# Preparation of a test-time-training layer: both channel swaps by on-chip transfers, the sine table in PSUM, key stores on ScalarE's queue, four target stores a batch

## Chip, cores and metric

The kernel runs on one core of a Trainium2 chip. The metric is the time of the device in microseconds (us), the median of several runs; lower is better. Engines are called PE (TensorE), DVE (VectorE), ACT (ScalarE), POOL (GpSimd) and SP (SyncE, which here only issues transfers).

## The reference, cut to what matters

The whole program is a small language-model tower on 4 sequences of 512 tokens, width 192: a token embedding, attention, a switch feed-forward layer, a test-time-training (TTT) layer, and a soft mixture of 32 experts. The change touches only what stands ahead of the TTT layer's recurrence. There, with 12 heads of 64 channels:

```python
xqk = x @ wq
XQ = causal_dwconv(xqk, conv_q_w, conv_q_b)      # 4 taps per channel
XK = causal_dwconv(xqk, conv_k_w, conv_k_b)
XV = x @ wv
XQ = rope(XQ, cos, sin)   # (x1*c - x2*s, x1*s + x2*c) on neighbouring channels
XK = rope(XK, cos, sin)
ttt_lr = sigmoid(x @ lr_w.T + lr_b)
# then a scan over mini-batches of 16 tokens, which uses XQ, XK, XV - XK and ttt_lr
```

## The kernel before, in words

The program is a row of blocks of engine programs; a block ends when all its engines have reached its end. `ttt_prepare` (lines 1070 to 1392) is one such block, between the switch layer and `ttt_recur` (from line 1395).

Channels lie on partitions, 128 at a time (2 heads of 64), and tokens along the free dimension, 512 at a time. A **unit** n is one group of 128 channels of one batch: 6 groups times 4 batches make 24 units, in order of batch and then group. All arithmetic is in fp32. For one unit, w = 1 is the key side and w = 0 the query side:

- PE, `project` (L1165): x.n, the projection of 512 tokens into one PSUM bank of two.
- ACT, `first_tap` (L1308, L1309): y1.n and y0.n, the oldest tap and the bias of the convolution, PSUM to SBUF.
- DVE, `tap` (L1238): the three other taps of each side, c1w.n to c3w.n, in place in `cy`. One operand is the PSUM bank of x.n, one is `cy` in SBUF.
- The rotation needs each channel's neighbour. For the keys PE multiplies by a pair-swapping matrix into PSUM (r1.n, L1217); for the queries SP issues two transfers within SBUF, one for the even and one for the odd partitions (`swap`, L1133), from `cy` into `rope_s`, 128 KB each.
- DVE, `partner`: the neighbour times the sine table, s1.n from PSUM (L1249) and s0.n in place in `rope_s` with the table in SBUF (L1244).
- POOL: m1.n and m0.n, `cy` times the cosine table (L1390); z1.n and z0.n, the sums, into `kT_all` and `qT_all` (L1380).
- PE, `target` (L1178 to L1180) and `turn_keys` (L1187): T.n, the target rows of the recurrence, 12 matmuls that need z1.n, and KT.n, four transposes of z1.n. Once a batch `rates` (L1198, L1199) adds eight narrow matmuls.
- ACT: kr.n copies the turned keys into `krows` (L1320, two instructions), rw.n copies the targets into `rows_` (L1334); both lie in the tensor called `t_late`. Once a batch ACT also takes the sigmoid of the rates.
- SP: two transfers store kr.n into DRAM (`k_d`, L1146, 256 KB each), and after the sixth unit of a batch eight transfers store `rows_` (`c_d`, L1152, 196 KB each). `rows_` has one buffer: rw of the next batch's first unit waits until all eight have landed (L1328, L1329).

The order of each engine is written out by hand, as software pipelining over a loop on n. In one turn DVE does c11.n, s1.(n-1), c10.n, c21.n, c20.n, c31.n, c30.n, s0.(n-1). PE does x.(n+1), T.(n-2), KT.(n-2), r1.n. POOL does z1.(n-1), m1.n, m0.n, z0.(n-1). ACT does y1.(n+1), y0.(n+1), kr.(n-2), rw.(n-2). SP issues the swap of n, then the stores of n-2. `y`, `rope_c`, `rope_s`, the banks of x and T, and `krows` have two buffers each; KT has one bank. So x.(n+1) waits for c30.(n-1), the swap of n waits for z0.(n-2), and y.(n+1) waits for the swap, r1 and the POOL product of unit n-1, since all read the buffer that it overwrites.

At the end PE runs five filling matmuls (L58) behind the last KT, and SP issues the last batch's eight stores. `ttt_recur` begins by loading its first target rows from `c_d` (L1454) and keys from `k_d` (L1457).

Of the kernel before, what the change touches and what calls it, by code (L numbers as in the profile page):

```python
# [15 lines left out]
P = 128  # L16
# [1053 lines left out]
def ttt_prepare(nc, M, ins, xT):  # L1070
    with ExitStack() as ctx:
# [11 lines left out]
                 for r in range(2)]  # L1083
        t15 = M["r_t15"]
        W0, B0, g2, mean0, blk = M["r_WB"][:, 0, :], M["r_WB"][:, 1, :], M["r_g2"], sb("p_mean0", [P, 2, HP]), M["blk"]
        ident, pair, ps, kT_all, qT_all = M["ident"], M["pair"], M["ps"], M["kT_all"], M["qT_all"]
        X, ROT, T, KT, LR = ps[0:2], ps[2:4], ps[4:6], ps[6], ps[7]
        t15_in, cleared, ones = (sem("p_" + n) for n in ("t15_in", "cleared", "ones"))
        start, centred = sem("p_start"), sem("p_centred")
        scaled, tabled, kept = sem("p_scaled"), sem("p_tabled"), sem("p_kept")  # L1090
# [1 line left out]
        swapped = [[sem(f"p_swap{w}{r}") for r in range(2)] for w in range(2)]  # L1092
        U = range(B * HP)
        END = len(U) - 1
        SWAPS = (0,)
        arrived = lambda w, n: (swapped[w][n % 2], 32 * (n // 2 + 1))
        q_of, p_of = (lambda n: n // HP), (lambda n: n % HP)
        rate_of = lambda n: n // HP
        dve = Steps(sem("p_dve"), [s for n in range(B * HP + 1) for s in
                                   ([f"c11.{n}"] if n in U else []) + ([f"s1.{n - 1}"] if n else [])  # L1100
                                   + ([f"c10.{n}", f"c21.{n}", f"c20.{n}", f"c31.{n}", f"c30.{n}"] if n in U else [])
                                   + ([f"s0.{n - 1}"] if n else [])])
        act = Steps(sem("p_act"), [f"y{w}.0" for w in (1, 0)] + [s for n in range(B * HP + 2) for s in
                    ([f"y1.{n + 1}", f"y0.{n + 1}"] if n + 1 in U else [])
                    + ([] if n - 2 not in U else [f"rw.{n - 2}", f"kr.{n - 2}"] if n - 2 == END else [f"kr.{n - 2}", f"rw.{n - 2}"]) + ([f"lr.{rate_of(n)}"] if n % HP == 3 else [])])
        pe = Steps(sem("p_pe"), ["x.0"] + [s for n in range(B * HP + 2) for s in
                   ([f"x.{n + 1}"] if n + 1 in U else []) + ([f"T.{n - 2}", f"KT.{n - 2}"] if n - 2 in U else [])
                   + ([f"lr.{rate_of(n)}"] if n % HP == 3 else [])
                   + ([f"r1.{n}"] if n in U else [])])
        pool = Steps(sem("p_pool"), [s for n in range(B * HP + 1) for s in  # L1110
                     ([f"z1.{n - 1}"] if n else []) + ([f"m1.{n}", f"m0.{n}"] if n in U else []) + ([f"z0.{n - 1}"] if n else [])])
        of = lambda b: slice(b * N, (b + 1) * N)
        tok = lambda b, t: slice(b * N + t * P, b * N + (t + 1) * P)
        z_of = lambda w, n: (kT_all if w else qT_all)[:, p_of(n), q_of(n), :]
        FIRST, REST = 16 * 2, 16 * 2 * (TB - 1)

        with nc.Block() as block:
            @block.sync
            def _(sp):
                for r in range(2):  # L1120
                    sp.sem_inc(kst[r], 1)
                sp.sem_inc(c_first, 1)
                sp.sem_inc(c_rest, 1)
                sp.dma_start(t15[:, :], ins["t_idx"][MB - 1:MB].rearrange("(a n) -> a n", a=1).to_broadcast([P, 1])).then_inc(t15_in, 16)
                sp.dma_start(M["xT_d"], xT[0:DC, :, :]).then_inc(kept, 16)
                for dst, src in ((W0, "t_W1"), (B0, "t_b1"), (g2[:, :], "t_g")):
                    sp.dma_start(dst, ins[src]).then_inc(start, 16)
                def swap(w, n):
                    sp.wait_ge(*dve.at(f"c3{w}.{n}"))
                    if n >= 2:  # L1130
                        sp.wait_ge(*pool.at(f"z{w}.{n - 2}"))
                    for a in range(2):
                        sp.dma_start(r2[a:P:2, n % 2, w, :], y[1 - a:P:2, n % 2, w, :]).then_inc(swapped[w][n % 2], 16)  # L1133

                for m in range(len(U) + 2):
                    if m in U:
                        for w in reversed(SWAPS):
                            swap(w, m)
                    if m < 2:
                        continue  # L1140
                    n = m - 2
                    b, p = q_of(n), p_of(n)
                    if n < END:
                        sp.wait_ge(*act.at(f"kr.{n}"))
                        for hh in range(2):
                            sp.dma_start(M["k_d"][b, hh, :, p * P:(p + 1) * P].rearrange("(t k) n -> k t n", t=TB),  # L1146
                                         krows[n % 2][:, :, hh, :]).then_inc(kst[n % 2], 16)
                    if p == HP - 1:
                        sp.wait_ge(*act.at(f"rw.{n}"))
                        for t in range(TB):  # L1150
                            for hh in range(2):
                                sp.dma_start(M["c_d"][b, hh, t * P:(t + 1) * P, :], rows_[:, t, hh, :]).then_inc(c_rest if t else c_first, 16)  # L1152
                sp.wait_ge(kept, 16)
                for w in SWAPS:
                    for r in range(2):
                        sp.wait_ge(*arrived(w, END - 1 + r))

            @block.tensor
            def _(t_):
# [43 lines left out]
                for n in range(len(U) + 2):  # L1203
                    if n + 1 in U:
                        if n:
                            t_.wait_ge(*dve.at(f"c30.{n - 1}"))
                        project(n + 1)
                    if n - 2 in U:
                        target(n - 2)
                        turn_keys(n - 2)  # L1210
                    if n % HP == 3:
                        rates(rate_of(n))
                    if n in U:
                        t_.wait_ge(*dve.at(f"c31.{n}"))
                        if n:
                            t_.wait_ge(*dve.at(f"s1.{n - 1}"))
                        t_.matmul(ROT[1], pair[:, :], y[:, n % 2, 1, :], start=True, stop=True).then_inc(*pe.did(f"r1.{n}"))  # L1217
                t_.wait_ge(*act.at(f"lr.{B - 1}"))
                fill(t_, LR, ident, 5)

# [1 line left out]
            def _(v):  # L1222
# [16 lines left out]
                        .then_inc(*dve.did(f"c{k}{w}.{n}"))  # L1239

                def partner(w, n):
                    if w in SWAPS:
                        v.wait_ge(*arrived(w, n))
                        v.tensor_tensor(r2[:, n % 2, w, :], r2[:, n % 2, w, :], rope[:, 1, :], ALU.mult).then_inc(*dve.did(f"s{w}.{n}"))  # L1244
                        return
                    v.wait_ge(*pe.at(f"r{w}.{n}"))
                    if n >= 2:
                        v.wait_ge(*pool.at(f"z{w}.{n - 2}"))
                    v.tensor_tensor(r2[:, n % 2, w, :], ROT[w], rope[:, 1, :], ALU.mult).then_inc(*dve.did(f"s{w}.{n}"))  # L1249

                for n in range(len(U) + 1):
                    if n in U:
                        tap(1, 1, n)
                    if n:
                        partner(1, n - 1)
                    if n in U:
                        tap(1, 0, n)
                        for k in (2, 3):
                            for w in (1, 0):
                                tap(k, w, n)  # L1260
                    if n:
                        partner(0, n - 1)
                    if n == 0:
                        v.wait_ge(scaled, 1)
# [35 lines left out]
            def _(a):  # L1300
                act.open(a)
                a.wait_ge(loaded, 112)
                a.activation(warm[:, :], cb[0][0:1, 0:1], ACT.Sigmoid).then_inc(tabled, 1)
                a.wait_ge(tabled, 1)

# [18 lines left out]
                def into_rows(n):  # L1324
# [5 lines left out]
                    if p == HP - 1:  # L1330
# [3 lines left out]
                    a.activation(rows_[:, :, :, p * E1:(p + 1) * E1], T[n % 2].rearrange("p (t a e) -> p t a e", t=TB, a=2),  # L1334
                                 ACT.Copy).then_inc(*act.did(f"rw.{n}"))

                def sigmoids(b):
                    a.wait_ge(*pe.at(f"lr.{b}"))
                    if b:
                        a.wait_ge(*act.at(f"rw.{b * HP - 1}"))  # L1340
                    a.activation(lrs[:, :], LR[:, 0:TB * H1], ACT.Sigmoid).then_inc(*act.did(f"lr.{b}"))
# [4 lines left out]
                for n in range(len(U) + 2):  # L1346
                    if n + 1 in U:
                        a.wait_ge(*pe.at(f"x.{n + 1}"))
                        if n:
                            for w in (1, 0):  # L1350
                                a.wait_ge(*(arrived(w, n - 1) if w in SWAPS else pe.at(f"r{w}.{n - 1}")))
                                a.wait_ge(*pool.at(f"m{w}.{n - 1}"))
                        for w in (1, 0):
                            first_tap(w, n + 1)
                    if n - 2 == END:
                        into_rows(END)
                        keys_into_rows(END)
                    elif n - 2 in U:
                        keys_into_rows(n - 2)
                        into_rows(n - 2)  # L1360
                    if n % HP == 3:
                        sigmoids(rate_of(n))
                a.wait_ge(*act.at(f"kr.{END}"))
# [5 lines left out]
            def _(g):  # L1369
# [10 lines left out]
                    g.tensor_tensor(z_of(w, n), r1[:, n % 2, w, :], r2[:, n % 2, w, :], ALU.add).then_inc(*pool.did(f"z{w}.{n}"))  # L1380

                for n in range(len(U) + 1):
                    if n:
                        rotated(1, n - 1)
                    if n in U:
                        for w in (1, 0):
                            g.wait_ge(*dve.at(f"c3{w}.{n}"))
# [1 line left out]
                                g.wait_ge(*pool.at(f"z{w}.{n - 2}"))  # L1389
                            g.tensor_tensor(r1[:, n % 2, w, :], y[:, n % 2, w, :], rope[:, 0, :], ALU.mult).then_inc(*pool.did(f"m{w}.{n}"))  # L1390
                    if n:
                        rotated(0, n - 1)


def ttt_recur(nc, M, ins):
    with ExitStack() as ctx:
# [49 lines left out]
        with nc.Block() as block:  # L1446
            @block.sync
            def _(sp):
# [20 lines left out]
                    sp.wait_ge(M["k_st"][r], 16 * B * HP + 1)  # L1469
                for r in range(RING):  # L1470
                    keys(r, r)
                sp.wait_ge(c_rest, 16 * 2 * (TB - 1) * B + 1)
                for dst, src in ((O["same"], ins["c_same"]), (O["prev"], ins["c_prev"]), (O["inv"], ins["c_inv"]),
                                 (O["idx"], ins["t_idx8"].rearrange("(a n) -> a n", a=1).to_broadcast([P, P]))):
                    sp.dma_start(dst[:, :], src).then_inc(O["masked"], 16)
# [143 lines left out]
            def _(v):  # L1619
# [6 lines left out]
                def aside(s, g):  # L1626
                    if s == 1:
                        v.wait_ge(M["c_st"][0], 16 * 2 * B + 1)
                        v.wait_ge(M["c_st"][1], 16 * 2 * (TB - 1) * B + 1)
                        v.memset(O["b6"][:, 2 * g:2 * g + 1, :, :], 0.0)  # L1630
                    if s == 2:
                        v.memset(O["b6"][:, 2 * g + 1:2 * g + 2, :, :], 0.0)
# [1110 lines left out]
```

## Time and profile before

| | us |
|---|---|
| median of 3 runs | 1338.97 (1336.88 to 1339.46) |
| the profiled execution's own time | 1341.67 |
| its span, first to last instruction | 1339.9 |
| busy in the span: PE, DVE, ACT, POOL | 1223.7, 927.6, 729.0, 387.8 |
| the preparation block, about | 356 to 522 of the span |

Rows of the timeline give the start, the duration, the engine, the line, what is written and read, and how many instructions are merged (x2 is two); in brackets the idle time ahead of it and what ended it. "SPq" and "ACTq" are the transfers issued by SP and ACT: their duration is that of issuing, not of moving the data. A matmul in fp32 appears as two PE instructions. Durations of neighbours on one engine overlap slightly, so the distance between two starts, not the duration, is what an instruction costs its engine.

### The profile page before, as it was taken

The numbers are of one execution on the slowest core, as the hardware profiler recorded it, in microseconds if no ns is written. First come the engines' busy times: TensorE is split into PE (matmuls) and PEld (weight loads), VectorE is DVE, ScalarE is ACT, GpSimd is POOL, SyncE is SP. The second block draws the span as 40 slices with busy tenths as digits, with TensorE's granted clock in tenths as the row PEclk, the third lists the DMA queues.
The fourth block names the chain that finished last, engine by engine and source line by source line (L and its number), as shares of the span: only waits on it lengthen the run. The fifth ranks groups of instructions, "written<-read, shape, count | busy, mean of one in ns | idle before, by whom it ended". The sixth has DMA issues, their size and how long they took to land. (4 is left out here: it accounts for less than half of the span.)

```text
span 1339.9 us, 29219 instructions
## 1 busy us (share of the span) xinstructions
PE 1223.7 (91%) x11303; PEld 850.2 (63%) x11303; DVE 927.6 (69%) x2303; ACT 729.0 (54%) x1529; POOL 387.8 (29%) x445
## 2 busy tenths in 40 slices
PE   5889999899689998999999988999976899899998
PEld 4533333346467776777777766787764455588888
DVE  7688888433799997898888868888864899300001
ACT  1446555442235454888888855888863344433310
POOL 7400000100178986556666630000000334200000
PEclk9989999999889999999999999999977999999999
DMA  4532121210225556434334522212004000277811
GB/s 104 138 96 71 49 60 37 57 33 1 73 87 182 175 182 199 135 97 131 122 108 135 144 85 60 60 42 66 24 1 193 34 1 0 72 274 278 281 57 47
DMA packets 103126, 133.71 MB, mean 100 GB/s; under 512 B 25357, under 2 KB 88572, under 8 KB 98796
## 3 DMA queue, kind: packets, MB, share of 16 engines
q1 hardware_dynamic: 100396, 129.73, 31.5%
q0 software_dynamic: 1536, 1.59, 0.5%
q8 instruction: 90, 1.47, 0.5%
q10 hardware_dynamic: 1056, 0.52, 0.1%
q14 instruction: 48, 0.39, 0.1%
HBM read 89.06 MB, written 37.88 MB: 95 GB/s over the span
## 5 line engine op out<-in xcount | busy, mean ns | idle before, releaser
L1832 POOL TENSOR_SCALAR r_grD<-gr 32x192 f32<-32x192 f32 x192 | 101.8, 530 | 95.3 <-PE bank L1563 48.7
L716 ACT ACTIVATE PT<-bank 128x1024 f32<-128x1024 f32 x96 | 94.2, 1022 | 59.3 <-PE bank L596 58.5
L657 DVE TENSOR_REDUCE mx<-bank 128x1 f32<-128x512 f32 x176 | 109.9, 681 | 12.0 <-PE bank L579 11.8
L2594 DVE TENSOR_TENSOR eo_all<-bank,m_b2s 128x768 f32<-128x768 f32 x8 | 7.7, 958 | 136.9 <-PE bank L2555 136.9
L1563 PE MATMUL bank<-r_grD,ek 128*128 128x256 f32 x384 | 100.0, 396 | 0.0
L2586 ACT ACTIVATE x_g<-bank,m_b1s 128x128 f32<-128x128 f32 x192 | 51.4, 400 | 75.7 <-PE bank L2537 75.7
L1390 POOL TENSOR_TENSOR rope_c<-cy,p_rope 128x512 f32<-128x512 f32 x48 | 70.9, 1499 | 19.1 <-DVE cy L1238 19.1
L2468 POOL TENSOR_SCALAR m_xs<-m_xs 128x256 f32<-128x256 f32 x4 | 2.5, 630 | 252.1 <-DVE m_xs L2359 251.3
L1563 PEld LDWEIGHTS bank<-r_grD,ek 128*128 128x128 f32 x384 | 67.7, 189 | 9.3
L1776 ACT ACTIVATE r_t<-r_xh,r_cd 128x64 f32<-128x64 f32 x192 | 70.0, 428 | 0.7
L1554 PEld LDWEIGHTS bank<-gr,r_A 128*128 128x128 f32 x384 | 47.7, 191 | 34.0 <-DVE gr L1726 32.8
L2478 POOL TENSOR_TENSOR m_cw<-m_E,m_f 128x512 f32<-128x512 f32 x32 | 47.4, 1500 | 63.0 <-DVE m_f L2400 59.2
L2555 PE MATMUL bank<-wb,x_g 128*32 128x192 f32 x1536 | 65.3, 327 | 0.0
L1554 PE MATMUL bank<-gr,r_A 128*128 128x64 f32 x384 | 56.3, 283 | 9.1 <-DVE gr L1726 6.6
L579 PE MATMUL bank<-K,Q 97*128 97x512 bf16 x176 | 60.1, 395 | 3.9 <-DVE mx L657 2.5
L1053 POOL MEMSET kT_all<- 1x2048 f32 x1 | 1.8, 1799 | 203.2 <-POOLq L541 203.2
L1805 POOL TENSOR_SCALAR KTz<-kT_all 64x384 f32<-64x384 f32 x68 | 57.1, 840 | 7.9 <-POOL r_grD L1832 5.0
L596 PE MATMUL bank<-Q,K 99*128 99x512 bf16 x192 | 58.1, 386 | 0.1
L1962 PE MATMUL bank<-o_xT,o_wg 96*128 96x256 f32 x192 | 48.1, 395 | 10.2 <-ACT o_gate L2115 10.2
L2555 PEld LDWEIGHTS bank<-wb,x_g 128*32 128x32 f32 x1536 | 48.5, 110 | 13.3
L1238 DVE SCALAR_TENSOR_TENSOR cy<-bank,p_cwk,cy 128x509 f32<-128x509 f32 (+2 forms) x72 | 53.0, 736 | 1.7 <-ACT cy L1309 1.7
L1238 DVE SCALAR_TENSOR_TENSOR cy<-bank,p_cwq,cy 128x509 f32<-128x509 f32 (+2 forms) x72 | 53.0, 736 | 0.0
(381 smaller groups left out, 3183.6 us busy)
## 6 DMA issues: line engine op xcount, KB each, us to landing
wb<-in_m_w SPq DMA_DIRECT2D x32, 1152.0 KB, 5.9
ek<-k_d SPq DMA_DIRECT2D x32, 384.0 KB
k_d<-t_late SPq DMA_DIRECT2D x46, 256.0 KB, 2.8
tgt<-c_d SPq DMA_DIRECT2D x33, 196.0 KB
c_d<-t_late SPq DMA_DIRECT2D x32, 196.0 KB, 3.0
rope_s<-cy SPq DMA_DIRECT2D x48, 128.0 KB, 2.1
g_d<-gr SPq DMA_DIRECT2D x32, 192.0 KB
o_G<-g_d SPq DMA_DIRECT2D x32, 192.0 KB, 3.1
```

The costliest lines, as they stand in the source:

```text
L579: t_.matmul(bank, Q[r][0:RA, hd, qt * P:(qt + 1) * P], K[r][0:RA, hd, :], start=True, stop=True)\
L596: last = t_.matmul(STB[s % 2][:, i, :], K[r][0:RB, hd, kt * P:(kt + 1) * P], Q[r][0:RB, hd, :], start=True, stop=True)
L657: v.tensor_reduce(mx[u % 2][:, j // 4, j % 4:j % 4 + 1], slot(f"A{u}.{j}"), AX.X, ALU.max).then_inc(*dve.did(f"max{u}.{j}"))
L716: a.activation(PT[kt % 2][:, 2 * hp:2 * hp + 2, :], STB[s % 2][:, :, :], ACT.Exp, scale=DH ** -0.5)\
L1238: v.scalar_tensor_tensor(yy, X[n % 2][:, 0:N - d], cw[w][:, p_of(n), k:k + 1], yy, ALU.mult, ALU.add)\
L1390: g.tensor_tensor(r1[:, n % 2, w, :], y[:, n % 2, w, :], rope[:, 0, :], ALU.mult).then_inc(*pool.did(f"m{w}.{n}"))
L1554: last = t_.matmul(Z[g][:, i * E1:(i + 1) * E1], A[g][:, i, :], gr[r][:, p * E1:(p + 1) * E1], start=False, stop=True, skip_group_check=True)
L1563: last = t_.matmul(SP_[g][:, i * B * E1:(i + 1) * B * E1], ek[r][:, p, :], grD[g][:, i, :, :].rearrange("p b e -> p (b e)"), start=False, ...
L1776: a.activation(t1[g][:, c], xh[g][:, c], ACT.Identity, bias=cd[g][:, 0, i:i + 1], scale=cd[g][:, 1, i:i + 1])\
L1805: return g_.tensor_scalar(KTz[r][rr, :, :, hh, :].rearrange("p h b k -> p (h b) k"), kT_all[rr, :, :, bass.ds(s * MB, MB)].rearrange("p h ...
L1832: last = g_.tensor_scalar(grD[g][rr, :, b, :], b3(gr[j % RING][rr, cols(g)]), 0.0, None, ALU.bypass)
L2555: last = t_.matmul(eo_bank(q, b)[i * S2:(i + 1) * S2, :], gT[(4 * q + i) % RG][:, c, b * S2:(b + 1) * S2], w[:, o:o + D], start=(c == 0 an ...
```

## The change

The key side is swapped by SP's transfers too, and r1 leaves PE. The sine table is copied once by ACT into PSUM bank 2, and both partner products read it there. DVE's turn becomes c11, c10, c21, c20, c31, c30 of n, then s1 and s0 of n-1; POOL's becomes m1, m0 of n, then z1, z0 of n-1. The two key stores of a unit are issued by ACT behind rw. The target rows of a batch are stored by four transfers: for each half one with the first 128 tokens and one with the other 384.

```diff
-        X, ROT, T, KT, LR = ps[0:2], ps[2:4], ps[4:6], ps[6], ps[7]
+        X, SINE, ROT, T, KT, LR = ps[0:2], ps[2], ps[2:4], ps[4:6], ps[6], ps[7]
...
-        SWAPS = (0,)
+        SWAPS = (0, 1)
...
-        FIRST, REST = 16 * 2, 16 * 2 * (TB - 1)
+        FIRST, REST = 16 * 2, 16 * 2
...
-                    if n < END:
-                        sp.wait_ge(*act.at(f"kr.{n}"))
-                        for hh in range(2):
-                            sp.dma_start(M["k_d"][b, hh, :, p * P:(p + 1) * P].rearrange("(t k) n -> k t n", t=TB),
-                                         krows[n % 2][:, :, hh, :]).then_inc(kst[n % 2], 16)
                     if p == HP - 1:
                         sp.wait_ge(*act.at(f"rw.{n}"))
-                        for t in range(TB):
+                        for t0, t1, done in ((0, 1, c_first), (1, TB, c_rest)):
                             for hh in range(2):
-                                sp.dma_start(M["c_d"][b, hh, t * P:(t + 1) * P, :], rows_[:, t, hh, :]).then_inc(c_rest if t else c_first, 16)
+                                sp.dma_start(M["c_d"][b, hh, t0 * P:t1 * P, :].rearrange("(t k) n -> k t n", k=P), rows_[:, t0:t1, hh, :])\
+                                    .then_inc(done, 16)
...
-                    if n in U:
-                        t_.wait_ge(*dve.at(f"c31.{n}"))
-                        if n:
-                            t_.wait_ge(*dve.at(f"s1.{n - 1}"))
-                        t_.matmul(ROT[1], pair[:, :], y[:, n % 2, 1, :], start=True, stop=True).then_inc(*pe.did(f"r1.{n}"))
...
                 def partner(w, n):
...
+                    v.wait_ge(*arrived(w, n))
+                    if n == 0:
+                        v.wait_ge(sined, 1)
+                    v.tensor_tensor(r2[:, n % 2, w, :], r2[:, n % 2, w, :], SINE, ALU.mult).then_inc(*dve.did(f"s{w}.{n}"))
...
                 a.wait_ge(loaded, 112)
+                a.activation(SINE, rope[:, 1, :], ACT.Copy).then_inc(sined, 1)
...
+                def store_keys(n):
+                    b, p = q_of(n), p_of(n)
+                    a.wait_ge(*act.at(f"kr.{n}"))
+                    for hh in range(2):
+                        a.dma_start(M["k_d"][b, hh, :, p * P:(p + 1) * P].rearrange("(t k) n -> k t n", t=TB),
+                                    krows[n % 2][:, :, hh, :]).then_inc(kst[n % 2], 16)
...
-                                a.wait_ge(*(arrived(w, n - 1) if w in SWAPS else pe.at(f"r{w}.{n - 1}")))
+                                a.wait_ge(*arrived(w, n - 1))
                                 a.wait_ge(*pool.at(f"m{w}.{n - 1}"))
...
                         keys_into_rows(n - 2)
                         into_rows(n - 2)
+                        store_keys(n - 2)
```

The written orders of DVE, PE and POOL follow the text above, and the recurrence's two waits on the target stores count four transfers a batch instead of eight.

## Rows read from the trace of the kernel before

**Rows 1.** Timeline of DVE, one turn of the steady stretch
```profile
430.70 0.73 DVE L1238 SCALAR_TENSOR_TENSOR cy<-bank,p_cwk,cy 128x509 f32<-128x509 f32 x1
431.36 0.67 DVE L1249 TENSOR_TENSOR rope_s<-bank,p_rope 128x512 f32<-128x512 f32 x1
431.95 0.73 DVE L1238 SCALAR_TENSOR_TENSOR cy<-bank,p_cwq,cy 128x509 f32<-128x509 f32 x1
...
435.23 1.32 DVE L1244 TENSOR_TENSOR rope_s<-rope_s,p_rope 128x512 f32<-128x512 f32 x1
436.48 0.73 DVE L1238 SCALAR_TENSOR_TENSOR cy<-bank,p_cwk,cy 128x509 f32<-128x509 f32 x1
```

**Rows 2.** Timeline of POOL, the same stretch
```profile
434.73 2.95 POOL L1390 TENSOR_TENSOR rope_c<-cy,p_rope 128x512 f32<-128x512 f32 x2 [0.37 <-DVE cy L1238]
437.64 1.27 POOL L1380 TENSOR_TENSOR qT_all<-rope_c,rope_s 128x512 f32<-128x512 f32 x1
```

**Rows 3.** Timeline of PE: one turn, then the rates of the first batch
```profile
436.74 1.88 PE L1165 MATMUL bank<-t_xT,p_wq 96*128 96x512 f32 x4
438.46 0.39 PE L1178 MATMUL bank<-p_wv,t_xT 96*128 96x128 f32 x2
...
441.57 1.02 PE L1217 MATMUL bank<-cy,pair 128*128 128x512 f32 x2
442.44 1.02 PE L1165 MATMUL bank<-t_xT,p_wq 96*128 96x512 f32 x2
...
386.79 0.26 PE L1198 MATMUL bank<-p_lrw,t_xT 96*128 96x12 f32 x1
...
388.47 1.10 PE L1217 MATMUL bank<-cy,pair 128*128 128x512 f32 x2
```

**Rows 4.** Timeline of ACT around the end of the second batch
```profile
448.33 0.60 ACT L1334 ACTIVATE t_late<-bank 128x512 f32<-128x512 f32 x1
...
457.33 0.60 ACT L1334 ACTIVATE t_late<-bank 128x512 f32<-128x512 f32 x1 [3.33 <-DMA c_d<-t_late]
458.03 0.20 ACT L1308 ACTIVATE cy<-p_cbk 128x4 f32<-128x4 f32 x1
...
459.56 0.83 ACT L1320 ACTIVATE t_late<-bank,r_t 128x256 f32<-128x256 f32 x2
```

**Rows 5.** Transfers: issues there (timeline of SP), ACT's two, and median landing
```profile
448.34 2.02 SPq L1146 DMA_DIRECT2D k_d<-t_late  x2
450.40 4.49 SPq L1152 DMA_DIRECT2D c_d<-t_late  x8
...
L1365 ACTq DMA_DIRECT2D k_d<-t_late x2: 412/489/566, 517.0 to 517.5; - x2
...
c_d<-t_late SPq DMA_DIRECT2D x32, 196.0 KB, 3.0
rope_s<-cy SPq DMA_DIRECT2D x48, 128.0 KB, 2.1
```

**Rows 6.** Windows: stretch, length, busy us and count by engine, PE clock, DMA share, GB/s
```profile
375.00:380.00 5.00, 5.00 (x23) 3.04 (x22) 5.00 (x7) 1.63 (x4) 5.00 (x6) 0.72 0.07 26
436.74:442.43 5.69, 5.69 (x35) 4.25 (x34) 5.69 (x9) 2.95 (x8) 5.33 (x5) 1.00 0.43 132
449.00:457.40 8.40, 8.40 (x54) 6.48 (x53) 8.40 (x13) 2.54 (x7) 8.02 (x7) 1.00 0.86 291
```

**Rows 7.** Timeline of DVE: the first tap of unit 1 and of unit 23
```profile
368.77 0.73 DVE L1238 SCALAR_TENSOR_TENSOR cy<-bank,p_cwk,cy 128x509 f32<-128x509 f32 x1
...
502.59 0.73 DVE L1238 SCALAR_TENSOR_TENSOR cy<-bank,p_cwk,cy 128x509 f32<-128x509 f32 x1
```

**Rows 8.** Timeline of the block's end: PE's filling, the last stores, the next block's first load
```profile
515.75 4.46 PE L58 MATMUL bank<-ident 128*128 128x512 f32 x10
516.27 5.42 SPq L1152 DMA_DIRECT2D c_d<-t_late  x8
522.34 1.38 SPq L1454 DMA_DIRECT2D tgt<-c_d  x2
```

More of the change, by code:

```diff
@@ L1086, in ttt_prepare @@
         ident, pair, ps, kT_all, qT_all = M["ident"], M["pair"], M["ps"], M["kT_all"], M["qT_all"]
-        X, ROT, T, KT, LR = ps[0:2], ps[2:4], ps[4:6], ps[6], ps[7]
+        X, SINE, ROT, T, KT, LR = ps[0:2], ps[2], ps[2:4], ps[4:6], ps[6], ps[7]
+        sined = sem("p_sined")
         t15_in, cleared, ones = (sem("p_" + n) for n in ("t15_in", "cleared", "ones"))
@@ L1099, in ttt_prepare @@
         dve = Steps(sem("p_dve"), [s for n in range(B * HP + 1) for s in
-                                   ([f"c11.{n}"] if n in U else []) + ([f"s1.{n - 1}"] if n else [])
-                                   + ([f"c10.{n}", f"c21.{n}", f"c20.{n}", f"c31.{n}", f"c30.{n}"] if n in U else [])
-                                   + ([f"s0.{n - 1}"] if n else [])])
+                                   ([f"c11.{n}", f"c10.{n}", f"c21.{n}", f"c20.{n}", f"c31.{n}", f"c30.{n}"] if n in U else [])
+                                   + ([f"s1.{n - 1}", f"s0.{n - 1}"] if n else [])])
         act = Steps(sem("p_act"), [f"y{w}.0" for w in (1, 0)] + [s for n in range(B * HP + 2) for s in
@@ L1107, in ttt_prepare @@
                    ([f"x.{n + 1}"] if n + 1 in U else []) + ([f"T.{n - 2}", f"KT.{n - 2}"] if n - 2 in U else [])
-                   + ([f"lr.{rate_of(n)}"] if n % HP == 3 else [])
-                   + ([f"r1.{n}"] if n in U else [])])
+                   + ([f"lr.{rate_of(n)}"] if n % HP == 3 else [])])
         pool = Steps(sem("p_pool"), [s for n in range(B * HP + 1) for s in
-                     ([f"z1.{n - 1}"] if n else []) + ([f"m1.{n}", f"m0.{n}"] if n in U else []) + ([f"z0.{n - 1}"] if n else [])])
+                     ([f"m1.{n}", f"m0.{n}"] if n in U else []) + ([f"z1.{n - 1}", f"z0.{n - 1}"] if n else [])])
         of = lambda b: slice(b * N, (b + 1) * N)
@@ L1241, in partner @@
                 def partner(w, n):
[L1242 to L1249, printed above, removed]
+                    v.wait_ge(*arrived(w, n))
+                    if n == 0:
+                        v.wait_ge(sined, 1)
+                    v.tensor_tensor(r2[:, n % 2, w, :], r2[:, n % 2, w, :], SINE, ALU.mult).then_inc(*dve.did(f"s{w}.{n}"))
                 for n in range(len(U) + 1):
                     if n in U:
[L1253 to L1258, printed above, removed]
+                        for k in (1, 2, 3):
                             for w in (1, 0):
@@ L1261, in _ @@
                     if n:
+                        partner(1, n - 1)
                         partner(0, n - 1)
@@ L1382, in _ @@
                 for n in range(len(U) + 1):
-                    if n:
-                        rotated(1, n - 1)
                     if n in U:
@@ L1391, in _ @@
                     if n:
-                        rotated(0, n - 1)
+                        for w in (1, 0):
+                            rotated(w, n - 1)
 def ttt_recur(nc, M, ins):
@@ L1471, in _ @@
                     keys(r, r)
-                sp.wait_ge(c_rest, 16 * 2 * (TB - 1) * B + 1)
+                sp.wait_ge(c_rest, 16 * 2 * B + 1)
                 for dst, src in ((O["same"], ins["c_same"]), (O["prev"], ins["c_prev"]), (O["inv"], ins["c_inv"]),
@@ L1628, in aside @@
                         v.wait_ge(M["c_st"][0], 16 * 2 * B + 1)
-                        v.wait_ge(M["c_st"][1], 16 * 2 * (TB - 1) * B + 1)
+                        v.wait_ge(M["c_st"][1], 16 * 2 * B + 1)
                         v.memset(O["b6"][:, 2 * g:2 * g + 1, :, :], 0.0)
```

## The prediction

> **What bounds the kernel now.** The blocks run one behind the other, so what the preparation block saves or loses reaches the end nearly whole. I read the timelines of its engines in the steady stretch first, then the windows, then the places where the regular pattern breaks: the end of a batch and of the block.
>
> The reader is to see two engines at their limit. DVE has no idle time in a turn, and a turn costs it 436.48 - 430.70 = 5.78 us [rows 1]: a tap costs 431.36 - 430.70 = 0.66 us, s1 (table in SBUF, neighbour in PSUM) 431.95 - 431.36 = 0.59, s0 (both in SBUF) 436.48 - 435.23 = 1.25. Six taps and two products make 6 x 0.66 + 0.59 + 1.25 = 5.80. PE is full as well: from x to x a turn is 442.44 - 436.74 = 5.70 us [rows 3], all of it busy [rows 6]. ACT is busy for 2.95 of 5.69 us, POOL for 5.33, of which part is waiting for DVE.
>
> Why s0 costs twice s1 is told by POOL's row. m1 begins at 434.73 and m0 behind it, 2.95 us for the two, where z0 takes 1.27 [rows 2]. Two undisturbed ones would take 2.54, so POOL loses 0.4 beside s0. So the two engines get in each other's way when DVE reads two SBUF operands. s1 and the taps, with one operand in PSUM, run beside POOL at 0.59 and 0.66.
>
> **The change, part by part.**
>
> *Sine table in PSUM.* Both products now read one SBUF and one PSUM operand, s1's kind: 0.59 each [rows 1]. DVE's turn becomes 6 x 0.66 + 2 x 0.59 = 5.14 us, 0.64 less. Bounds: nothing saved if the in-place form kept 1.25 (the taps, in place as well, speak against it), 0.66 at most per product. The copy of the table costs ACT one instruction of rw's kind, 0.60 us [rows 4], once, while PE makes the first projection; bounds 0 and 0.6. I take 0.
>
> *r1 leaves PE.* It costs 442.44 - 441.57 = 0.87 us a turn [rows 3], so PE's turn falls to 5.70 - 0.87 = 4.83, and 388.47 - 386.79 = 1.68 for the rates once in six, 5.11 on the mean. PE stays just below DVE and works through every turn.
>
> *POOL* has four instructions of 1.27: 5.08 us at most [rows 2], no longer lengthened. It is just below DVE too. In the new order z follows both m, and z1.(n-1) now starts two products (2.5 us) behind c31.n; T.(n-1) waits for it, but PE has x.(n+1) to do meanwhile.
>
> *Swap of the keys.* SP issues four transfers a turn where it issued two, and two fewer stores. Issuing takes about 0.5 us each [rows 5], 2.2 us of 5.14, so SP is not the bound. The queries' swap is issued behind the keys', and lands about 2 x 0.55 + 2.1 = 3.2 us behind c30 [rows 5]. What waits is y of two units on (it overwrites what the swap reads), and c11 behind it: 1.53 us for the two y (459.56 - 458.03) [rows 4]. That is 4.7 us, and c11 comes 1.2 + 5.14 = 6.3 us behind that c30. So the transfer is hidden with 1.6 us to spare; with 3 us more landing time it would not be.
>
> *Key stores on ACT.* ACT now does two y (1.53), kr (0.73), rw (0.60) and two issues of 0.49 [rows 4, 5]: 3.84 us of 5.14. But these stand in one chain: c30.(n-1) lets x.(n+1) start, 438.46 - 436.74 = 1.72 us [rows 3], but T.(n-2) behind it waits for z1.(n-2), the third POOL product after c31.(n-1): 3 x 1.27 - 0.66 = 3.2 us. Then come T and KT, 441.57 - 438.46 = 3.1, kr and rw 1.3, the stores 1.0, y 1.5 and six taps 3.96, to the end of c30.(n+2): 14.1 us, some 0.3 more for hand-overs, for three turns of 15.4. One microsecond is left in three turns. The bounds of a store pair are 0.98, ACT's own pair, and 2.02, SP's in the crowded stretch [rows 5]; I take 1.0 and keep the other for a rival.
>
> *Steady sum.* 22 turns from c11.1 to c11.23 now take 502.59 - 368.77 = 133.82 us [rows 7], 6.7 more than 22 x 5.78 = 127.2. The 6.7 are PE's slow start at half clock (0.72) [rows 6] and the ends of batches. The new turns take 22 x 5.14 = 113.1, and I keep the 6.7.
>
> *Ends of batches.* ACT's rw of the next batch waits until all target stores have landed: 457.33 - 448.33 = 9.0 us after the last rw, of which 3.33 are idle [rows 4]. In that stretch the DMA engines are busy for 0.86 of the time, against 0.43 in an ordinary turn [rows 6], so it is mostly the volume that sets the landing, and issuing four transfers instead of eight, and 2 us earlier because the keys no longer go ahead, gives little. An ordinary turn uses 0.43 x 5.69 = 2.45 us of all DMA engines for 768 KB; the second swap adds 256 KB, 0.8 us by bytes. So I let the 9.0 stand, bounds 6.5 (the 2.5 us of issuing saved whole) and 10. Due is the rw after one turn, 5.14 instead of 5.7 us, so ACT waits 3.9 us where it waited 3.33, and what follows there is longer: the store pair stands ahead of y. DVE, which now loses about a microsecond at such a place, loses about 3: 1.8 us more at each of three, 5.4 in all (bounds: -3 and +9).
> The Trainium skill (Trainium Kernel Development and Optimization, the rules on DMA) says that transfers issued from several queues run on the same 16 engines, and that issuing from several only saves the sequencers' time. By it the key stores on ACT bring nothing in this crowded stretch; if issue time set the landing instead, the sum would be rival A's. The share of 0.86 is on the rule's side.
>
> So c11.1 to c11.23 takes 113.1 + 6.7 + 5.4 = 125.2 us, 8.6 less.
>
> *Tail.* Behind the last taps POOL has five instructions ahead of the end of z1.23, instead of four of which two are lengthened: +0.5 us (bounds 0 and 0.9). The block's end is set by SP's eight stores, 516.27 + 5.42 = 521.69, behind which the next block's first load is issued at 522.34 [rows 8]. Four stores of 0.56 end by 518.5, and then PE's filling is last, 515.75 + 4.46 = 520.21: 1.5 us saved (bounds 0, if the first target rows then land as late as now, and 2).
>
> *Sum.* -8.6 + 0.5 - 1.5 = -9.6 us. The profiled execution took 1341.67 us (span 1339.9 and 1.8 around it), so it would take 1332.1. The median of the runs is 2.7 below it, 1338.97, and gives 1329.4. I say 1329.
>
> **The rivals.**
>
> *A: the ends of batches hide, and DVE sets all turns.* If four transfers, issued 2 us earlier, land 2.5 us earlier, the wait is 1.4 us instead of 3.3 and vanishes in ACT's slack. Then 113.1 + 3 to 6 us of losses, 15 to 18 less, and 1.0 for the tail: 1321 to 1323. For it: less issuing. Against it: the DMA share of 0.86, and 0.8 us more of swaps. Chance 0.17.
>
> *B: ACT's chain becomes the bound.* If a store pair costs ACT 2.0 us [rows 5] and swaps and key stores, now on two queues, slow each other, the chain is 15.5 to 16.4 us for three turns, 5.3 on the mean, and the ends of batches cost another microsecond: 22 x 5.3 + 6.7 + 8.4 = 131.7, 2 less, with the tail 3: about 1336. For it: SP's pairs of stores often took 1.8 to 2 us beside target stores. Against it: nothing shows such times in ordinary turns. Chance 0.2.
>
> *C, slower: PE's clock.* Granted clock 0.72 at 375 to 380 [rows 6] means that PE ran at its lower level (1.2 instead of 2.4 GHz) for 0.56 x 5 = 2.8 us, after PE had stood mostly idle. r1 is what keeps PE full now. When T waits at the ends of batches PE would stand still for some 3 us, and a turn at the lower level costs up to 9.7 instead of 4.8. If each of the three ends is followed by two turns at half clock, that is 3 x 2 x (9.7 - 5.14) = 27 us more, hence 1329 + 27 less some overlap: about 1350. It decides from about 10 us lost, one slow turn at two ends or more. Against it: steady turns leave PE 94% busy, and it worked through the ends of batches before (8.40 of 8.40) [rows 6]. Chance 0.08.
>
> *D, slower: the product does not get cheaper.* If s keeps 1.25 although its table lies in PSUM, DVE's turn is 6 x 0.66 + 2.5 = 6.46, 22 x 0.68 = 15 us more: 1354. Against it: s1's 0.59 beside a busy POOL. Chance 0.04.
>
> **How the numbers follow.** The forecast has 0.51: a gain of 7 to 12 us by the bounds of its terms. A 0.17, B 0.2, C 0.08, D 0.04. The range goes from 1320 (A with all of its gain) to 1336 (B): it leaves out C, D and a part of B. No change means within 0.2%, 2.7 us, about what a measurement of this kernel can tell from none: the worse third of B, and mild forms of C, 0.08. Slower: most of C and D, 0.11. Faster: 0.81.
>
> **What would show it.** In the changed profile: both products at about 0.68 us duration, POOL's m pairs at 2.5 instead of 2.95, no L1217. DVE's turn in the steady stretch at 5.1 to 5.2 us without idle time; at 5.3 or more, with c11 waiting for ACT, it is B. ACT's wait on the target stores at three places: about 4 us is my reading, under 2 is A. PE's clock at 1.00 from 385 on, or C. The first load of the recurrence 9 to 10 us sooner than 522.34, with the same time from there to the end. I am wrong if DVE waits in ordinary turns, or if the recurrence or the experts take another time than before.

## The result, and the profile after

| | kernel before | changed kernel |
|---|---|---|
| median of 4 runs | 1338.04 us | 1324.89 us (1323.35 to 1325.79) |
| ratio, 95% interval | | 0.9905 [0.9885, 0.9924] |
| the profiled execution, its span | 1341.67, 1339.9 | 1325.54, 1323.8 |
| second group of runs of the changed kernel | 1336.96 | 1325.97 us, 0.9913 [0.9881, 0.9945] |

The kernel became 13.2 us faster. I had said 9.6 less, 1329, in a range of 1320 to 1336. (The forecast started from a median before of 1338.97, of three runs; with the fourth it is 1338.04.)

DVE's and POOL's timelines of the changed kernel, one turn of the steady stretch (it answers to [rows 1, 2]):

```profile
393.12 0.74 DVE L1228 SCALAR_TENSOR_TENSOR cy<-bank,p_cwk,cy 128x509 f32<-128x509 f32 x1
...
397.06 1.27 DVE L1235 TENSOR_TENSOR rope_s<-rope_s,bank 128x512 f32<-128x512 f32 x2
398.25 0.74 DVE L1228 SCALAR_TENSOR_TENSOR cy<-bank,p_cwk,cy 128x509 f32<-128x509 f32 x1
...
396.56 2.51 POOL L1379 TENSOR_TENSOR rope_c<-cy,p_rope 128x512 f32<-128x512 f32 x2 [0.15 <-DVE cy L1228]
```

The two products take 398.25 - 397.06 = 1.19 us together, 0.59 each, and POOL's pair 2.51 instead of 2.95. A DVE turn is 398.25 - 393.12 = 5.13 us.

PE's turn, without the swap (to [rows 3]):

```profile
394.06 1.88 PE L1160 MATMUL bank<-t_xT,p_wq 96*128 96x512 f32 x4
...
398.89 1.45 PE L1160 MATMUL bank<-t_xT,p_wq 96*128 96x512 f32 x3
```

From x to x it is 398.89 - 394.06 = 4.83 us here, as summed.

The waits between 376 and 507 us, in total, times and longest:

```profile
ACT cy L1291 <- DMA rope_s<-cy: 16.8, 12, 3.9
ACT t_late L1317 <- DMA c_d<-t_late: 10.2, 3, 4.5
DVE cy L1228 <- ACT cy L1292: 4.9, 6, 1.1
DVE rope_s L1235 <- DMA rope_s<-cy: 4.3, 4, 2.2
```

DVE waits 9.2 us in that stretch: 6.9 around the three ends of batches, for a swap that has not landed or for ACT, which waits for the swap itself, 0.95 behind the first rates, and 1.3 behind the last unit. ACT's three waits on the target stores make 10.2 us, against 10.1 before.

Windows, with the columns of [rows 6]: the start, a steady turn, the end of the second batch.

```profile
360.00:370.00 10.00, 3.78 (x4) 1.17 (x4) 10.00 (x18) 1.63 (x4) 2.62 (x3) 0.58 0.39 131
370.00:375.00 5.00, 4.51 (x9) 2.39 (x10) 5.00 (x9) 0.69 (x2) 4.81 (x5) 0.50 0.27 105
375.00:380.00 5.00, 5.00 (x34) 4.04 (x34) 5.00 (x9) 2.29 (x7) 4.96 (x4) 0.97 0.31 117
...
394.40:399.60 5.20, 5.20 (x34) 4.06 (x33) 5.20 (x10) 3.32 (x9) 5.05 (x5) 1.00 0.62 204
...
438.60:447.70 9.10, 9.03 (x66) 7.41 (x65) 7.40 (x12) 2.60 (x8) 8.77 (x8) 1.00 0.89 306
```

The DMA share is 0.62 in a plain turn (I had 0.63) and 0.89 at an end. PE's clock is low for longer at the start than before, and 1.00 in the two later windows. It falls once more at the end of the block: from 488.0 to 491.3, behind c11.23, PE is busy for 1.60 of 3.30 us, and from 491.3 to 494.7 its granted clock is 0.51. In the kernel before PE is busy for all of 488 to 495, at 1.00.

The end of the block and the first rates of the recurrence (to [rows 8]), first of the kernel before, one row that was not shown:

```profile
526.36 0.16 DVE L1671 TENSOR_TENSOR r_rl<-r_rs,tgt 128x3 f32<-128x3 f32 x1 [0.85 <-DMA tgt<-c_d]
```

and of the changed kernel:

```profile
502.05 4.46 PE L58 MATMUL bank<-ident 128*128 128x512 f32 x10
502.57 1.90 SPq L1146 DMA_DIRECT2D c_d<-t_late  x4
506.90 2.13 SPq L1444 DMA_DIRECT2D tgt<-c_d  x2
513.56 0.18 DVE L1661 TENSOR_TENSOR r_rl<-r_rs,tgt 128x3 f32<-128x3 f32 x1 [3.49 <-DMA tgt<-c_d]
```

PE's filling is now the last work of the block, but the first rates, which wait for the first target rows, come 6.7 us after the issue of their load instead of 4.0.

**Sections of a profile.** The timeline lets the block be measured by itself, from the first tap of unit 1 to that of unit 23, to the first load, to the first rates, to the end:

| us | c11.1 to c11.23 | to first load | to first rates | block | to the end |
|---|---|---|---|---|---|
| before | 133.82 | 19.75 | 4.02 | 157.6 | 813.5 |
| changed | 122.06 | 18.42 | 6.66 | 147.1 | 810.2 |
| changed, second profile | 122.75 | 18.40 | 6.60 | 147.8 | 810.6 |

Each row is one profile. The stretch ahead of c11.1 is nearly the same code in all kernels here, and took from 364 to 380 us in the profiles of this study. So whole times of single runs compare badly, and I read the experiments by these sections as well as by their medians.

### The profile page after: what moved, and what is told of

Read it like the earlier page. It is cut to its first block and busy times, and to the rows that moved or that the text cites. A ratio compares the mean times of both kernels' runs of the same rounds, so it can differ in the third digit from the quotient of the medians.

```text
span 1323.8 us, 29136 instructions
## 1 busy us (share of the span) xinstructions
PE 1204.3 (91%) x11255; PEld 839.2 (63%) x11255; DVE 913.4 (69%) x2303; ACT 728.9 (55%) x1530; POOL 374.4 (28%) x445
## 5 line engine op out<-in xcount | busy, mean ns | idle before, releaser
L1379 POOL TENSOR_TENSOR rope_c<-cy,p_rope 128x512 f32<-128x512 f32 x48 | 60.0, 1271 | 23.3 <-DVE cy L1228 23.3
L1160 PE MATMUL bank<-t_xT,p_wq 96*128 96x512 f32 x96 | 49.3, 640 | 11.1 <-DVE cy L1228 9.7
L1952 PE MATMUL bank<-o_xT,o_wg 96*128 96x256 f32 x192 | 48.1, 395 | 10.1 <-ACT o_gate L2105 10.1
```

## Experiments

**1. The table back in SBUF**, the rest as changed:

```diff
-                    v.tensor_tensor(r2[:, n % 2, w, :], r2[:, n % 2, w, :], SINE, ALU.mult)
+                    v.tensor_tensor(r2[:, n % 2, w, :], r2[:, n % 2, w, :], rope[:, 1, :], ALU.mult)
```

> The changed kernel, but both partner products read the sine table in SBUF again. My theory (two SBUF operands on DVE and a running POOL instruction hold each other up): each product waits for POOL, a DVE turn goes from 5.14 to about 6.4 us (6 x 0.66 + 2 x 1.25), POOL's four to more than 5.1, 22 turns cost 25 to 30 us more than in the changed kernel: 1350 to 1355 us, slower than the kernel before. Rival: the gain came from taking the swap off PE, and the table's place costs little (a turn of 5.2 to 5.5, under 1332).

Measured: 1354.73 us, ratio 1.0115 [1.0083, 1.0148]; c11.1 to c11.23 148.7 us, a turn of 6.86. The timelines of POOL and DVE:

```profile
441.58 2.95 POOL L1379 TENSOR_TENSOR rope_c<-cy,p_rope 128x512 f32<-128x512 f32 x2 [1.01 <-DVE cy L1228]
...
442.08 3.00 DVE L1235 TENSOR_TENSOR rope_s<-rope_s,p_rope 128x512 f32<-128x512 f32 x2
...
444.49 1.71 POOL L1371 TENSOR_TENSOR kT_all<-rope_c,rope_s 128x512 f32<-128x512 f32 x1
445.00 0.74 DVE L1228 SCALAR_TENSOR_TENSOR cy<-bank,p_cwk,cy 128x509 f32<-128x509 f32 x1
```

The pair of products costs DVE 445.00 - 442.08 = 2.92 us, not 1.19, and POOL loses 0.4 us in the pair and again in the next instruction (1.71). They take turns: POOL's first product ends at 442.85 and DVE's first at 443.40, POOL's second at 444.53 and DVE's second at 445.08. In the first turns of the same run it is POOL alone that pays: DVE's pair takes 376.86 - 375.66 = 1.20 us, and POOL's product that began at 375.16 takes 2.90. What decides between the two patterns the trace does not show. All that changed is the memory of one operand. So with both swaps as transfers, the table's place decides in the block's rows between 10.5 us less than before (147.1) and 17.3 more (174.9). The forecast of the whole time, 1350 to 1355, came out; the size of the turn was off: I had put 6.4 us, with two products of 1.25.

**2. The table alone**, on the kernel before:

```diff
-                        v.tensor_tensor(r2[:, n % 2, w, :], r2[:, n % 2, w, :], rope[:, 1, :], ALU.mult)
+                        v.tensor_tensor(r2[:, n % 2, w, :], r2[:, n % 2, w, :], SINE, ALU.mult)
```

> The kernel before, with nothing changed but the sine table of the queries' product in PSUM. DVE's sum falls to 5.14 us a turn, but PE still needs 5.70 and 1.7 for the rates once a batch. My theory: PE is right behind DVE, so the turn stays at 5.70 and DVE waits 0.55 in each: 0 to 3 us faster than before (1335 to 1338). Rival: PE's 5.70 is elastic and DVE alone set the turn: 10 us faster or more.

Measured: 1336.00 us, ratio 0.9985 [0.9969, 1.0001]; steady turns of 5.69 to 5.70 us, c11.1 to c11.23 133.8, as before. DVE waits for r1 in each turn:

```profile
440.00 0.69 DVE L1252 TENSOR_TENSOR rope_s<-bank,p_rope 128x512 f32<-128x512 f32 x1 [0.47 <-PE bank L1218]
```

**3. PE filled again**: a matmul of r1's size, for nothing, in each turn of the changed kernel.

```diff
                     if n % HP == 3:
                         rates(rate_of(n))
+                    if n in U:
+                        fill(t_, ROT[1], ident, 1)
```

> The changed kernel, with one matmul of the removed swap's size (0.87 us, its result unused, waiting for nothing) back on PE in each turn. If PE's room decides, the turn is 5.70 us and six tenths of the change's gain in the block are gone: 22 x 0.56 = 12 us above the changed kernel, 1335 to 1338. Rival: PE had room and DVE alone gave the gain: within 2 us of the changed kernel (1323 to 1327).

Measured: 1336.64 us, ratio 0.9989 [0.9967, 1.0011]; steady turns of 5.69 us, c11.1 to c11.23 132.6. DVE's wait moved to ACT's first taps, which wait for x:

```profile
426.90 0.75 DVE L1230 SCALAR_TENSOR_TENSOR cy<-bank,p_cwk,cy 128x509 f32<-128x509 f32 x1 [0.49 <-ACT cy L1294]
```

Experiments 2 and 3 fit together: both relieve DVE and leave PE full, and in both that is worth nothing in the turn beyond the 0.09 us by which PE's turn is shorter. The opposite half, PE relieved and DVE's turn left at 5.78, was not run, since a swap by transfer gives DVE a second product from SBUF; experiment 1 is the nearest to it, and there DVE's turn grew to 6.86. Of what was run, only both together give the turn of 5.13.

**4. Keys stored by SP again**: L1146's loop back in SP's program, `store_keys` no longer called.

```diff
+                    if n < END:
+                        sp.wait_ge(*act.at(f"kr.{n}"))
+                        for hh in range(2):
+                            sp.dma_start(M["k_d"][b, hh, :, p * P:(p + 1) * P].rearrange("(t k) n -> k t n", t=TB),
...
-                        store_keys(n - 2)
```

> The changed kernel with the key stores issued by SP again, ahead of the target stores. My theory: DVE sets the turn (5.13) either way; at the three ends of batches ACT is freed of 1 us but the target stores are issued 1 to 2 us later: within 2 us of the changed kernel, 1323 to 1327. Rival B (ACT's chain matters): 2 to 5 us faster. Other rival (SP's queue was the reason to move them): swaps behind stores arrive late in ordinary turns, DVE waits, 3 to 8 us slower than the changed kernel.

Measured: 1328.65 us, ratio 0.9934 [0.9909, 0.9958], an interval that overlaps the changed kernel's; c11.1 to c11.23 123.0 us, the block 146.7. In the block there is no difference to the changed kernel's 147.1 and 147.8. The median lies 1.7 us above the band that I gave and in that of the other rival, late swaps. The profile speaks against this rival: the plain turns take 5.13 to 5.14 us, and the swaps hold DVE up only near the ends. But it is of one of the fastest runs (1322.42, in a spread of 1322 to 1336), so what made the others longer stays open. In that profile it does not matter which queue the keys go by.

**5. The changed kernel again**, as the measure of the next three.

> The changed kernel itself, once more, beside the others of this group: 1323 to 1327 us if its first runs were typical; the comparisons of this group are made against it.

Measured: 1325.97 us, as said.

**6. Eight target stores a batch**:

```diff
-                        for t0, t1, done in ((0, 1, c_first), (1, TB, c_rest)):
+                        for t0, t1, done in [(t, t + 1, c_rest if t else c_first) for t in range(TB)]:
```

> The changed kernel with eight target stores a batch instead of four. My theory (the volume sets when they land): ACT's wait at the three ends of batches stays at 3 to 4.5 us; at the block's end SP issues 2.5 us longer, which is where PE's filling ends anyway, so the next block begins 0 to 1.5 us later, but its first load waits less than 3.5 us behind the smaller stores: within 2 us of the changed kernel. Rival A: the number of issues sets the landing, each end costs 2 us more: 5 to 8 us slower than the changed kernel.

Measured: 1330.07 us, ratio 0.9946 [0.9927, 0.9964]; the block 148.4 us. In the sections: 1.4 us more up to c11.23, 1.8 more to the first load, 2.6 less to the first rates (4.0 us again), in sum 0.7 more than experiment 5. The medians differ by 4.1, twice what I allowed, of which the block shows 0.7; the rest stays open. Rival A's 2 us at each end are not there. ACT's three waits on the target stores sum to 10.2 us with eight as with four.

**7. Targets in halves**: the columns of the first three units stored behind the third, by two transfers; ACT waits at units 0 and 3 of a batch for the part that it overwrites.

```diff
+                    if p == HP // 2 - 1:
+                        sp.wait_ge(*act.at(f"rw.{n}"))
+                        for hh in range(2):
+                            sp.dma_start(M["c_d"][b, hh, :, 0:HALF // 2].rearrange("(t k) n -> k t n", k=P), rows_[:, :, hh, 0:HALF // 2])\
+                                .then_inc(c_part, 16)
```

> The changed kernel with the target rows of a batch stored in two parts: the columns of the first three units right behind the third, the rest behind the sixth; ACT waits at each part for its own stores, three turns old. My theory (ends of batches cost DVE 8 us in all, because 1.57 MB go at once): ACT's waits on target stores vanish, the turns at the ends fall to 5.2 to 5.6 us, 5 to 8 us faster than the changed kernel: 1317 to 1321. Rival (the DMA engines are near their limit on the mean, or ACT's and SP's issues are what is late): under 2 us faster.

Measured: 1326.56 us, ratio 0.9922 [0.9894, 0.9950]; c11.1 to c11.23 120.9 us, the block 144.8, 3.0 less than experiment 5. No median shows that, and the 1317 to 1321 that I had expected did not come; by its time the rival was right. ACT's waits on the target stores are gone, as said, but two waits stay:

```profile
ACT cy L1297 <- DMA rope_s<-cy: 18.7, 10, 3.3
DVE rope_s L1241 <- DMA rope_s<-cy: 5.8, 4, 3.2
```

and behind the start five turns are long, of 5.9 to 7.0 us, where experiment 5 had three of 7.0 to 8.7. So the buffer was only half of it: the swaps are late too. Half the stores at the block's end bring the first rates 3.8 us behind the load.

**8. The recurrence's first load on ACT's queue**:

```diff
                 act.open(a)
+                a.wait_ge(M["c_st"][0], 16 * 2 * B + 1)
+                for r in range(RING):
+                    a.dma_start(tgt[r][:, :], M["c_d"][:, :, r * MB:(r + 1) * MB, :].rearrange("b h k n -> (b h) k n")).then_inc(tgt_in[r], 16)
```

> The changed kernel, with the first two loads of target rows in the recurrence issued from ACT's queue instead of SP's. Theory: they were late (3.5 us of waiting on DVE) because on SP's queue they stand behind 1.2 MB of stores still moving; on the other queue they land 2 to 3 us sooner, and the end comes 1.5 to 3 us sooner. Rival: all queues share the same engines and the loads wait as long: no difference.

Measured: 1328.69 us, ratio 0.9927 [0.9899, 0.9956]. From load to first rates 5.4 us instead of 6.6, and DVE no longer waits for the transfer; but the block takes 147.5, and the median is 2.7 above experiment 5's. The two issues (2.1 us) now stand ahead of ACT's own first work there, and the rates wait for that, so 5.4 is no measure of the transfer. Nor does it set this queue apart: with the same four stores and the load on SP's queue, experiments 3 and 4 also came to 5.3. Inconclusive on the reason, and no improvement.

**9 to 11. Which queue delays the swaps?** Target stores issued by ACT, behind `store_keys`: whole (9), in halves (10), in halves with the keys on SP (11).

```diff
-                    if p == HP - 1:
+                    if n == END:
                         sp.wait_ge(*act.at(f"rw.{n}"))
...
                         store_keys(n - 2)
+                        store_targets(n - 2)
```

> The changed kernel, with the four target stores of the first three batches issued by ACT behind the key stores, instead of by SP ahead of the next swaps. Theory F (what stops DVE at the ends of batches is that the swaps stand behind 1.57 MB of stores on SP's own queue): DVE's waits on the swap go, but ACT now spends 2 to 3 us more in issuing and still waits for its buffer, so DVE's losses at the three ends change from 8 us in all to 5 to 8. Theory G (only the volume matters, whatever the queue): the same swaps are as late, and ACT's issuing comes on top: 10 us or more of losses.

Measured: 1335.57 us beside 1343.73 for the kernel before, ratio 0.9934 [0.9908, 0.9960]; c11.1 to c11.23 126.6 us. Its waits:

```profile
ACT cy L1291 <- DMA rope_s<-cy: 19.4, 7, 7.1
DVE cy L1228 <- ACT cy L1292: 11.9, 10, 2.2
DVE rope_s L1235 <- DMA rope_s<-cy: 0.8, 1, 0.8
```

ACT's longest wait, 7.1, belongs to the start, where the changed kernel waits as long, ahead of the stretch that its 16.8 us cover. The 12.3 that are left stand beside those 16.8. DVE's own waits on the swap are nearly gone, as theory F has it, but ACT's are not, and DVE waits for ACT instead. The losses, 126.6 - 113.0 = 13.6 us, of which the start has 1.7, are theory G's.

> Target rows stored in two parts (columns of three units each), issued by ACT instead of SP, so that no store at all stands ahead of a swap on SP's queue until the last batch. Theory F: neither the buffer nor the swap is late, c11.1 to c11.23 takes 116 to 118 us (113.0 plus the start's 1.2 and some of ACT's issuing), 3 to 5 less than with the two parts on SP. Theory G: the same 121 as with the two parts on SP, or more by ACT's issuing.

Measured: 1332.41 us, ratio 0.9915 [0.9888, 0.9941]; c11.1 to c11.23 121.8 us where F wanted 116 to 118 and G 121 or more. F has fallen: taking the stores off the swaps' queue alone does not bring the swaps in time.

> The same, with the key stores on SP's queue again, so that ACT issues only target stores. If ACT's issuing is what is left, c11.1 to c11.23 takes a microsecond or two less than with both on ACT (115 to 117). If the swaps are delayed by any store ahead of them on their own queue, it takes 1 to 3 us more.

Measured: 1325.63 us, ratio 0.9867 [0.9838, 0.9896]; c11.1 to c11.23 119.7 us, the block 142.6. It is 2.2 less than with both on ACT, so ACT's issuing is part of what is left there; 115 to 117 was too low.

**12. That version once more**:

> The last version once more, in more rounds, for its ratio to the kernel before. From the block alone (c11.1 to the recurrence's first rates 142.6 us, against 147.1 and 147.8 in two profiles of the changed kernel and 157.6 before) I expect it 14 to 16 us below the kernel before, a ratio of 0.988 to 0.990, and 4 to 5 us below the changed kernel. If the first group's 0.987 was luck of the stretch ahead of the block, the ratio comes out at 0.990 or more.

Measured: 1325.96 us beside 1343.91, 18 us below it where I had said 14 to 16; ratio 0.9856 [0.9824, 0.9889]; the block 142.2 us. In the block it is 4.5 to 5.5 us ahead of the changed kernel. A lead in whole time is not shown: the two were not run in one group, their medians are alike (1325.96 and 1325.97, beside 1343.91 and 1336.96 for the kernel before), and the intervals of the ratios overlap a little ([0.9881, 0.9945] for the changed kernel). What remains is still a wait for the swaps: in this last profile ACT waits 26.3 us for them in 12 places, 7.2 of it at the start, which leaves 19.1.

## Why the prediction was right, and where it was off

- **What bounds the block.** Right: two engines at 5.78 and 5.70 us a turn, and experiments 2 and 3 show that relieving DVE alone gives nothing. But over a batch the two were not level: PE needed 6 x 5.70 + 1.68 = 35.9 us with the rates, DVE 6 x 5.78 = 34.7. I did not draw that sum, and it comes back under the ends of batches.
- **The table in PSUM.** Right: 0.59 per product, 5.13 a turn for 5.14. The Trainium skill (SBUF — State Buffer, Who interferes with whom) says that a DVE instruction with two SBUF inputs contends with a GpSimd instruction that reads SBUF, and one with at most one does not. Experiment 1 agrees: 2.92 us against 1.19 for the pair.
- **r1 leaves PE**: 4.83 as summed. Rival C did not come where it was looked for: the low stretch was at the start, 0.50 to 0.58 up to 375, and then the granted clock stayed at 1.00 past c11.23, all three ends of batches included. It came in a mild form behind that, from 491.3 to 494.7, and cost nothing that the rows show: from c11.23 to the first load the changed kernel took 18.42 us, experiment 3, whose clock stayed at 1.00 there, 18.41.
- **The steady sum** was mis-sized at "and I keep the 6.7". Before, 3.5 of these 6.7 us lay in the three turns from c11.2 to c11.5, which took 6.60, 6.77 and 7.48 us; in the changed kernel they took 5.14, 5.13 and 6.16, a loss of 1.0. PE ran at half clock until 377.8, only the first of the three, and fell behind; at full clock it had no room to catch up, and DVE waited 0.25, 0.90 and 1.60 us for r1, the last time behind the rates. r1 is gone. That is 2.5 of the 3.1 us by which c11.1 to c11.23 came out under my 125.2. Experiment 3, where PE has work of that size again, bears it out in part: 5.13, 5.75 and 7.48 us.
- **Ends of batches.** Near in size, 3.2 (the rest of the 6.7) plus 5.4 said and 8.0 measured (turns of 7.46, 5.46, 8.68, 5.48 and 6.58, and small ones), but in part by luck. The kept 3.2 were mostly not the stores'. In the kernel before, the turns in which ACT waited for the first two batches' stores took 5.79 and 5.87 us; the long ones, 7.03 and 6.94, come right behind them, where r1 stands behind the rates:

```profile
425.56 0.69 DVE L1249 TENSOR_TENSOR rope_s<-bank,p_rope 128x512 f32<-128x512 f32 x1 [1.16 <-PE bank L1217]
...
461.50 0.69 DVE L1249 TENSOR_TENSOR rope_s<-bank,p_rope 128x512 f32<-128x512 f32 x1 [1.06 <-PE bank L1217]
```

Only at the third end did the swap and ACT cost DVE 1.0 us. In the changed kernel the turns behind the later rates take 5.14 us: that loss went with r1. So the ends cost about 7 us more than before where I had put 5.4 more, and about 2.5 us of PE's loss went that I had kept.

ACT's waits on the stores were 3.1, 4.5 and 2.7 us, not 3.9 each. The reason was incomplete too: I had only the buffer of the target rows in it; experiment 7 took that wait away and the swaps were late as well. For the swap I had noted that 3 us more landing time would not be hidden, and had not applied it to the ends. That neither the number of the issues (experiment 6) nor the queue (experiments 4, 9 and 10) removes the wait agrees with the rule that the prediction quotes from the Trainium skill (Trainium Kernel Development and Optimization, Key Constraints); that the volume does it is the reading left over, and experiment 7, the same volume in two parts, moved the wait and did not end it. Rival A is out: it needed the waits to shrink, and they stayed at 10.2 us with four stores and with eight.
- **ACT's chain (B).** Not seen: a store pair cost 0.93 us in plain turns, and no plain turn waited. Taking the pair off ACT gained nothing in the block (experiment 4). It gained 2.2 us only where ACT also issues the target stores (experiment 11 against 10).
- **Tail.** To the first load 1.3 us less, 1.0 said. I had not put in that the first rates would come later behind their load: 2.6 us more. Eight smaller stores take that back (experiment 6), and so do halves (7); with the same four stores it was 1.3 in experiments 3 and 4, so the stores' size is not all of it.
- **The whole block.** 10.5 us less where the sum had 9.6: near, but two misses cancel, 3.1 us too little in the loop and 2.3 too much in the tail.
- **The rest.** The block gives 10.5 us of the medians' 13.2. From the first rates to the end, unchanged code took 813.5 us before and 810.2 after, and 808 to 813 in the experiments. I had named another time of the recurrence or the experts as a sign of being wrong; with one profile of the kernel before, these 3.3 us can't be told from scatter, and it stays open.

## What to carry to other kernels

When two engines have nearly the same length of turn, cost both before relieving one, with the work that comes only once in some turns: relieving DVE alone measured as nothing, twice. Where DVE and POOL work side by side, put one of two operands of a DVE product into PSUM if a bank is free. Storing in parts spread over the loop took 3 to 5.5 us off the block here, where the number of stores made 0.7; look also at which transfer waits behind a store. And the section that a change touches is better measured by its own rows than by the whole time, when code ahead of it scatters by more than the effect.

## What the runs showed of the hardware that I had not expected

- With two SBUF operands on both, DVE and POOL alternate instruction by instruction in the steady turns: 1.46 us per product instead of 0.59, and two of POOL's four instructions take 1.7 us instead of 1.27 (experiment 1).
- Behind two stores of 196 KB and two of 588 KB, issued over 1.9 us, the first rates came 6.6 to 6.7 us after the issue of their load of 196 KB on the same queue in the changed kernel, but 5.3 in experiments 3 and 4; behind eight of 196 KB, issued over 5.4 us, it was 4.0 (experiment 6).
